# Other start bytes for the stationary operands of a gated feed-forward stage, and for half of its moving ones

## The chip, the cores and the metric

The kernel runs on one core of one Trainium2 chip. The metric is the device time of one execution in microseconds (us), the median of several runs. The profile is one profiled execution of the same program.

## The reference, cut to what matters

The input `x` has 2 x 1024 tokens of 256 numbers. Four blocks follow each other, each added to `x`: a cross attention of one head over 154 context rows, a dense feed-forward stage with eight experts, a cross attention of eight heads, and a routed feed-forward stage with eight experts. The stage that the change touches is the second:

```python
def expert_step(acc, w):          # w: Wg (256 x 1024), Wu (256 x 1024), Wd (1024 x 256) of one expert
    wg, wu, wd = w
    h = jax.nn.silu(x @ wg) * (x @ wu)
    return (acc + h @ wd, None)
acc, _ = jax.lax.scan(expert_step, jnp.zeros_like(x), (Wg, Wu, Wd))   # 8 experts, all tokens
x = x + jnp.tanh(g_ffn[0]) * acc
```

All of it is float32.

## The kernel before

**Tiling.** The 1024 inner columns of each expert are cut into four quarters of 256, which makes 32 quarters in all, and the 2048 tokens into two pairs of 1024. A quarter with a pair is a group: 64 groups, numbered `n`, run one after the other, mostly both pairs of a quarter in a row. Gate and up (`X` is "g" or "u") of a group are not the eight block products each that the plain scheme needs, but seven (`product1` to `product7`) of sums of blocks. The weight blocks and their sums stand in `w_hi` and `w_lo` (two sets, used by even and odd quarters, written by GpSimd), the token blocks and their sums in `xop_hi` and `xop_lo` (one set for each pair, written once).

**Three matmuls for one product.** Each float32 operand is split into a high part rounded to float32r and the rest, and a product is three float32r matmuls of 128x128 by 128x512, from the function `three`:

```python
mm(ps, w, a, ...)        # L1400  high stationary, high moving
mm(ps, w, a_low, ...)    # L1401  high stationary, low moving
mm(ps, w_low, a, ...)    # L1402  low stationary, high moving
```

Each `mm` becomes a load of the stationary operand (LDWEIGHTS, PEld in the profile) and a MATMUL that streams the moving operand. In 64 groups, gate and up take 14 products each, that is 896 products. `down` and `down_seven` multiply the hidden blocks by `Wd`: 484 products, whose stationary operands are `wd_hi` and `wd_lo` (two sets again) or, in 28 groups that use seven products here too, also `wds_hi` and `wds_lo`; the moving ones are `hid_hi` and `hid_lo`, of which even groups use set 0 and odd groups set 1, and `t_hi`, `t_lo`. Together this is 1380 products and 4140 matmuls of one shape.

**Other engines.** VectorE adds halves, multiplies gate by up, subtracts for `hid_lo` and adds the results of down into `acc`. ScalarE applies silu, moves halves and rounds `hid_hi`. GpSimd prepares the weights of the next quarter while the present one is multiplied. SyncE issues the loads. TensorE's order is written out by hand in a loop over `n`, in which the steps of down for group `n - 1` stand between the products of group `n`.

**Places in memory.** Tiles are laid out by `Arena.take`, which gives each a start at the next multiple of 32 bytes in every partition. `align(OPERANDS_AT)` goes on to the next multiple of 2048. In the kernel before, every stationary and every moving operand of the 4140 matmuls begins at a multiple of 64 bytes, and every moving one at a multiple of 2048, since the sizes of all tiles between them are multiples of 2048 or of 512. The stationary operands of the query projection in the third block, `Wq_hi` and `Wq_lo`, are float32r too, and begin 32 bytes behind a multiple of 64; their moving operands `xnT_hi` and `xnT_lo` begin at multiples of 2048 (L1577, L1578, L1582, 96 matmuls of the same shape).

Of the kernel before, what the change touches and what calls it, by code (L numbers as in the profile page):

```python
# [16 lines left out]
F32 = mybir.dt.float32  # L17
F32R = mybir.dt.float32r
# [7 lines left out]
P = 128  # L26
# [63 lines left out]
def flamingo_kernel(nc, x, ctx, mask, g_xattn, g_ffn, W0, b0, Wg, Wu, Wd, gamma, beta, Wq, Wkv, Wout, wgate, We, be, out):  # L90
    B, S, D = x.shape
# [86 lines left out]
    with ExitStack() as stack:  # L178
# [5 lines left out]
        end = nc.sbuf_usable_end // 32 * 32  # L184
# [68 lines left out]
        st = Arena(nc, keep.at, sums_at)  # L253
# [1 line left out]
        half12 = {X: st.take(f"half12_{X}", [P, CH], F32) for X in "gu"}  # L255
        half22 = {X: st.take(f"half22_{X}", [P, CH], F32) for X in "gu"}
        hid = {h: st.take(f"hid{h}", [P, CH], F32) for h in BLOCKS[:2]}
        hid_hi, hid_lo = [], []
        st.align(OPERANDS_AT)
        for i in range(2):  # L260
            hid_hi.append({h: st.take(f"hid_hi{h}_{i}", [P, CH], F32R) for h in BLOCKS})
            if i == 0:
                t3_at = st.at + 4 * CH * BLOCKS.index("12")
            hid_lo.append({h: st.take(f"hid_lo{h}_{i}", [P, CH], F32R) for h in BLOCKS})
# [17 lines left out]
        sb = Arena(nc, sums_at, end)  # L282
# [7 lines left out]
            xop_lo.append(sb.take(f"xop_lo{p}", [P, 7, CH], F32R))  # L290
        xop_end = sb.at
        w_at, w_hi, w_lo, w_raw, wd_hi, wd_lo = [], [], [], [], [], []
        for i in range(2):
            w_at.append(sb.at)
            w_hi.append(sb.take(f"w_hi{i}", [P, 2, 7, P], F32R))
            w_raw.append(Arena(nc, sb.at, end).take(f"w_raw{i}", [P, 2, 7, P], F32))
            w_lo.append(sb.take(f"w_lo{i}", [P, 2, 7, P], F32R))
            wd_hi.append(sb.take(f"wd_hi{i}", [P, 2, D], F32R))
            wd_lo.append(sb.take(f"wd_lo{i}", [P, 2, D], F32R))
        raw_at = sb.at  # L300
        raw_gu = [sb.take(f"raw_gu{i}", [P, 2, KB, FP], F32) for i in range(2)]
        raw_d = [sb.take(f"raw_d{i}", [P, 2, D], F32) for i in range(2)]
# [2222 lines left out]
```

## Time and profile before

| | us |
|---|---|
| median of 3 runs | 1226.97 (1226.01 to 1227.29) |
| the profiled execution's span | 1225.2 |
| TensorE busy | 1199.5 (98%) |
| VectorE busy | 1051.4 (86%) |
| GpSimd busy | 886.6 (72%) |
| ScalarE busy | 739.6 (60%) |
| TensorE's weight loads busy | 987.8 (81%) |

The span runs from the first instruction to the last; the execution's own time beside it is 1226.97 - 1225.2 = 1.8 us longer, going by the median of the runs. A busy MATMUL is counted from its start to its modelled end, which overlaps the next one's start, so its duration is longer than the distance between starts. The distance between two starts is called a step below.

The first attention takes the first 54 us of the span, the dense feed-forward stage from 54 to 999 us, and the last two blocks the rest.

### The profile page before, as it was taken

What the parts mean: (1) busy time and instruction counts of PE and PEld (TensorE: products, weight loads), DVE (VectorE), ACT (ScalarE), POOL (GpSimd) and SP (SyncE); (2) the same over time, 40 slices, a digit from 0 to 9 for tenths busy, and PEclk for the clock granted to TensorE, in tenths of its full rate; (3) what the DMA queues carried; (4) which work ended last, traced back from release to release, by engine and by line L of the source; (5) the groups of instructions that cost most, each with busy time, mean ns of one, the idle gap of its engine ahead of it and who ended that gap; (6) DMA issues with size and microseconds to landing.
All of it is one profiled execution on the core that took longest, in us unless ns stands there. A gap on an engine that the chain in (4) does not pass through costs nothing.

```text
span 1225.2 us, 18428 instructions
## 1 busy us (share of the span) xinstructions
PE 1199.5 (98%) x6143; PEld 987.8 (81%) x6143; DVE 1051.4 (86%) x1754; ACT 739.6 (60%) x1531; POOL 886.6 (72%) x848
## 2 busy tenths in 40 slices
PE   8999999999999999999999999999999998999998
PEld 6778888888888888888888888888888887777776
DVE  6887899999999999999999999999999874767556
ACT  4775566666666666666666666666666545545544
POOL 4575688888888888878888888888888626444435
PEclk9999999999999999999999999999999999999999
DMA  4020301000000000000000000011000330000131
GB/s 142 26 95 25 98 13 39 27 26 26 27 26 27 26 27 26 27 26 27 27 26 27 26 27 26 27 38 40 27 26 1 120 121 1 19 26 11 36 96 70
DMA packets 42365, 48.27 MB, mean 39 GB/s; under 512 B 4239, under 2 KB 40143, under 8 KB 42015
## 3 DMA queue, kind: packets, MB, share of 16 engines
q1 hardware_dynamic: 38992, 43.33, 10.7%
q0 software_dynamic: 1440, 3.41, 0.7%
q8 instruction: 49, 0.80, 0.3%
q10 hardware_dynamic: 1839, 0.37, 0.2%
q14 instruction: 45, 0.37, 0.1%
HBM read 37.36 MB, written 10.29 MB: 39 GB/s over the span
## 4 chain that ended last, share of the span: by engine, by line
PE 89%; DVE 5%; ACT 3%; issue 1%; ACTq 1%; POOL 0%; POOLq 0%; DVEq 0%
PE bank L1400 25%; PE bank L1402 25%; PE bank L1401 25%; ACT PC L1124 3%; PE bank L1643 2%; PE bank L1652 1%; PE bank L1822 1%; DVE nmC L2204 1%; PE bank L1805 1%; PE bank L1345 1%; PE bank L1755 1%; DVE stats L1879 1%; PE bank L1577 1%; PE bank L1627 1%; PE bank L1578 1%
## 5 line engine op out<-in xcount | busy, mean ns | idle before, releaser
L1400 PE MATMUL bank<-xop_hi,w_hi 128*128 128x512 f32 x896 | 349.2, 390 | 1.9 <-DVE half_g L2028 0.9
L1402 PE MATMUL bank<-xop_hi,w_lo 128*128 128x512 f32 x896 | 348.6, 389 | 0.0
L1401 PE MATMUL bank<-xop_lo,w_hi 128*128 128x512 f32 x896 | 348.6, 389 | 0.0
L2063 DVE TENSOR_TENSOR hid_lo<-hid,hid_hi 128x512 fp32r<-128x512 f32 x228 | 232.5, 1044 | 6.0 <-ACT hid_hi L1042 6.0
L1400 PEld LDWEIGHTS bank<-xop_hi,w_hi 128*128 128x128 f32 x896 | 168.2, 188 | 37.9 <-DVE half_g L2028 1.3
L1402 PEld LDWEIGHTS bank<-xop_hi,w_lo 128*128 128x128 f32 x896 | 168.2, 188 | 35.0
L1401 PEld LDWEIGHTS bank<-xop_lo,w_hi 128*128 128x128 f32 x896 | 168.2, 188 | 34.7
L1042 ACT CAST hid_hi<-hid 128x512 fp32r<-128x512 f32 x228 | 140.8, 622 | 63.6 <-PE bank L1402 38.3
L1026 ACT ACTIVATE s<-bank 128x512 f32<-128x512 f32 x128 | 78.2, 611 | 95.2 <-PE bank L1402 95.2
L1400 PE MATMUL bank<-hid_hi,wd_hi 128*128 128x512 f32 x344 | 134.2, 390 | 0.7 <-DVE hid_lo L2063 0.6
L1401 PE MATMUL bank<-hid_lo,wd_hi 128*128 128x512 f32 x344 | 133.9, 389 | 0.0
L1402 PE MATMUL bank<-hid_hi,wd_lo 128*128 128x512 f32 x344 | 133.9, 389 | 0.0
L1002 ACT COPY bank<-bank 128x512 f32<-128x512 f32 x128 | 73.2, 573 | 67.9 <-PE bank L1402 67.9
L2087 DVE TENSOR_TENSOR acc<-bank,acc 128x512 f32<-128x512 f32 x136 | 93.0, 684 | 20.4 <-PE bank L1402 20.3
L1032 ACT ACTIVATE half_g<-half_g 128x512 f32<-128x512 f32 x128 | 81.1, 634 | 46.8 <-DVE half_g L2036 25.5
L2055 DVE TENSOR_TENSOR hid<-half_u,half_g 128x512 f32<-128x512 f32 x128 | 107.2, 875 | 0.0
L702 POOL TENSOR_TENSOR t_loT<-t_rawT,t_hiT 128x512 fp32r<-128x512 f32 x56 | 84.2, 1526 | 16.4 <-ACT t_hiT L1049 16.4
L2046 DVE TENSOR_TENSOR hid<-bank,s 128x512 f32<-128x512 f32 x128 | 86.6, 676 | 1.2 <-PE bank L1402 1.2
L648 POOL TENSOR_TENSOR w_lo<-w_raw,w_hi 128x1024 fp32r<-128x1024 f32 x32 | 77.5, 2421 | 2.9 <-ACT w_hi L1063 2.9
L796 POOL TENSOR_TENSOR PC<-PC,rdenC 128x616 f32<-128x616 f32 x32 | 38.9, 1216 | 53.5 <-DVE rdenC L2212 53.4
L1400 PEld LDWEIGHTS bank<-hid_hi,wd_hi 128*128 128x128 f32 x344 | 64.6, 188 | 15.3 <-DVE hid_lo L2063 1.0
L1402 PEld LDWEIGHTS bank<-hid_hi,wd_lo 128*128 128x128 f32 x344 | 64.6, 188 | 13.5
(288 smaller groups left out, 2608.3 us busy)
## 6 DMA issues: line engine op xcount, KB each, us to landing
raw_gu<-in_L_ffn_Wg_dram SPq DMA_DIRECT2D x32, 256.0 KB, 2.7
raw_gu<-in_L_ffn_Wu_dram SPq DMA_DIRECT2D x32, 256.0 KB, 3.1
raw_d<-in_L_ffn_Wd_dram SPq DMA_DIRECT2D x32, 256.0 KB, 3.6
slots<-empty_row SPq DMA_DIRECT2D x1, 2080.0 KB, 11.2
xr<-slots SPq DMA_DIRECT2D x8, 260.0 KB, 4.5
x_res<-in_x_dram SPq DMA_DIRECT2D x4, 512.0 KB, 8.9
x_mid<-x_res SPq DMA_DIRECT2D x1, 2048.0 KB, 7.4
x_res<-x_mid SPq DMA_DIRECT2D x4, 512.0 KB, 5.4
```

The lines of the kernel that those rows point to most:

```text
L648: nc.gpsimd.tensor_tensor(out=lo[:, :, W_S1:W_S4 + 1], in0=s[:, :, W_S1:W_S4 + 1], in1=hi[:, :, W_S1:W_S4 + 1].bitcast(F32), op=ALU.subtra ...
L702: nc.gpsimd.tensor_tensor(out=t_lo[i][:], in0=t_raw[i][:], in1=t_hi[i][:].bitcast(F32), op=ALU.subtract).then_inc(t_ready, 1)
L1026: nc.scalar.activation(out[:], ps[:], ACT.Silu).then_inc(silu_ready[h], 1)
L1032: nc.scalar.activation(half["g"][:], half["g"][:], ACT.Silu).then_inc(silu_ready[h], 1)
L1042: nc.scalar.copy(hid_hi[n % 2][h][:], hid[h][:]).then_inc(hi_ready[h], 1)
L1400: mm(ps, w, a, start=start, stop=False, skip_group_check=True)
L1401: mm(ps, w, a_low, start=False, stop=False, skip_group_check=True)
L1402: return mm(ps, w_low, a, start=False, stop=True, skip_group_check=True)
L2046: nc.vector.tensor_tensor(out=hid[h][:], in0=ps[:], in1=s[:], op=ALU.mult).then_inc(hid_ready[h], 1)
L2055: nc.vector.tensor_tensor(out=hid[h][:], in0=half["u"][:], in1=half["g"][:], op=ALU.mult).then_inc(hid_ready[h], 1)
L2063: nc.vector.tensor_tensor(out=hid_lo[n % 2][h][:], in0=hid[h][:], in1=hid_hi[n % 2][h][:].bitcast(F32), op=ALU.subtract).then_inc(lo_ready ...
L2087: nc.vector.tensor_tensor(out=to, in0=ps, in1=to, op=ALU.add).then_inc(acc_added, 1)
```

## The change

No instruction is added, removed or moved on any engine, and no semaphore. Tiles begin at other bytes.

- `w_hi`, `w_lo` and `w_raw` are taken with a few elements more: a start of 4 or 12 elements (`HI_AT`) or 8 or 0 (`LO_AT`), and 2 elements (8 bytes) between the gate half and the up half (`SIDE_PAD`).
- `wd_hi` and `wd_lo` get starts of 0 or 2 (`D_HI_AT`) and 12 or 1 elements (`D_LO_AT`).
- `hid_hi` and `hid_lo` of set 1 begin 32 bytes later (`MOVING_AT`).

What this makes of the starts, in bytes modulo 64, worked out from the arena (number of matmuls in brackets):

| stationary tile | before | after |
|---|---|---|
| w_hi, both sets, gate / up (1792) | 0 | 16 / 24 |
| w_lo of set 0, gate / up (448) | 0 | 0 / 8 |
| w_lo of set 1, gate / up (448) | 0 | 32 / 40 |
| wd_hi of set 0 / set 1 (372 / 372) | 0 | 32 / 8 |
| wd_lo of set 0 / set 1 (186 / 186) | 0 | 16 / 36 |
| wds_hi, wds_lo (336) | 0 | 0 |

Moving operands: `xop` (2688 matmuls) and `hid` of set 0 and `t` (684) stay at a multiple of 2048; `hid` of set 1 (768) goes to 32 bytes behind one. Behind the weights everything moves on by 160 to 320 bytes: `raw_gu`, `raw_d`, and in the later blocks `k1T`, `Wouts`, `Wkvs`, `Wqs`, `be_hl` and the routing tiles. `Wq_hi`, `Wq_lo` and the `xnT` tiles stay.

```diff
-        hid_hi, hid_lo = [], []
+        hid_hi, hid_lo, MOVING_AT = [], [], (0, 32)
         st.align(OPERANDS_AT)
         for i in range(2):
+            st.at += MOVING_AT[i]
             hid_hi.append({h: st.take(f"hid_hi{h}_{i}", [P, CH], F32R) for h in BLOCKS})
...
         w_at, w_hi, w_lo, w_raw, wd_hi, wd_lo = [], [], [], [], [], []
+        HI_AT, LO_AT, SIDE_PAD = (4, 12), (8, 0), 2
+        D_HI_AT, D_LO_AT = (0, 2), (12, 1)
+
+        def sides(arena, name, dt, first):
+            n = 7 * P + SIDE_PAD
+            flat = arena.take(name, [P, first + 2 * n], dt)
+            return flat[:, first:first + 2 * n].rearrange("p (s n) -> p s n", s=2)[:, :, 0:7 * P].rearrange("p s (b c) -> p s b c", b=7)
+
+        def down_blocks(arena, name, first):
+            flat = arena.take(name, [P, first + 2 * D], F32R)
+            return flat[:, first:first + 2 * D].rearrange("p (f d) -> p f d", f=2)
+
         for i in range(2):
             w_at.append(sb.at)
-            w_hi.append(sb.take(f"w_hi{i}", [P, 2, 7, P], F32R))
-            w_raw.append(Arena(nc, sb.at, end).take(f"w_raw{i}", [P, 2, 7, P], F32))
-            w_lo.append(sb.take(f"w_lo{i}", [P, 2, 7, P], F32R))
-            wd_hi.append(sb.take(f"wd_hi{i}", [P, 2, D], F32R))
-            wd_lo.append(sb.take(f"wd_lo{i}", [P, 2, D], F32R))
+            w_hi.append(sides(sb, f"w_hi{i}", F32R, HI_AT[i]))
+            w_raw.append(sides(Arena(nc, sb.at, end), f"w_raw{i}", F32, LO_AT[i]))
+            w_lo.append(sides(sb, f"w_lo{i}", F32R, LO_AT[i]))
+            wd_hi.append(down_blocks(sb, f"wd_hi{i}", D_HI_AT[i]))
+            wd_lo.append(down_blocks(sb, f"wd_lo{i}", D_LO_AT[i]))
```

## Rows read from the trace of the kernel before

**Rows 1.** The page: busy us (share of the span) and instructions of each engine; the granted clock.

```profile
PE 1199.5 (98%) x6143; PEld 987.8 (81%) x6143; DVE 1051.4 (86%) x1754; ACT 739.6 (60%) x1531; POOL 886.6 (72%) x848
...
PEclk9999999999999999999999999999999999999999
```

**Rows 2.** Busy time of each engine by window, all of the span, then granted clock.

```profile
core 0: us, PE busy (x) PEld busy (x) DVE busy (x) ACT busy (x) POOL busy (x), PEclk, DMA share, GB/s
...
484.90:514.14 29.24, 29.24 (x130) 24.21 (x129) 27.32 (x37) 18.56 (x34) 24.48 (x23) 1.00 0.09 28
...
200.00:800.00 600.00, 600.00 (x2649) 496.82 (x2648) 559.76 (x740) 380.39 (x676) 503.07 (x454) 1.00 0.09 28
```

**Rows 3.** The chain that ended last, by line, as shares of the span.

```profile
by line: PE bank L1400 25.4%; PE bank L1402 25.3%; PE bank L1401 25.3%; ACT PC L1124 2.6%; PE bank L1643 1.7%; PE bank L1652 1.5%; PE bank L1822 1.1%; issue 1.1%; DVE nmC L2204 1.0%; PE bank L1805 1.0%; PE bank L1345 0.7%; PE bank L1755 0.7
```

**Rows 4.** Timeline of TensorE: start us, us, line, operation, tiles.

```profile
499.65 0.39 PE L1400 MATMUL bank<-hid_hi,wd_hi 128*128 128x512 f32 x1
499.87 0.39 PE L1401 MATMUL bank<-hid_lo,wd_hi 128*128 128x512 f32 x1
...
514.61 0.39 PE L1400 MATMUL bank<-hid_hi,wds_hi 128*128 128x512 f32 x1
```

**Rows 5.** Timeline of the weight loads beside them.

```profile
499.65 0.19 PEld L1401 LDWEIGHTS bank<-hid_lo,wd_hi 128*128 128x128 f32 x1
499.88 0.19 PEld L1402 LDWEIGHTS bank<-hid_hi,wd_lo 128*128 128x128 f32 x1
```

**Rows 6.** Line 1401 from 200 to 900 us: duration ns min/median/max.

```profile
L1401 PE MATMUL bank<-xop_lo,w_hi x671: 389/389/389, 200.0 to 899.0; 128*128 128x512 f32 x168
L1401 PE MATMUL bank<-hid_lo,wd_hi x240: 389/389/389, 206.1 to 897.7; 128*128 128x512 f32 x120
```

**Rows 7.** The same for lines of the query projection, whole span.

```profile
L1578 PE MATMUL bank<-xnT_hi,Wq_lo x32: 392/396/398, 1014.4 to 1141.7; 128*128 128x512 f32 x32
L1582 PE MATMUL bank<-xnT_lo,Wq_hi x32: 387/396/397, 1017.9 to 1143.6; 128*128 128x512 f32 x32
```

**Rows 8.** Timeline of TensorE in the first query projection.

```profile
1014.38 0.40 PE L1578 MATMUL bank<-xnT_hi,Wq_lo 128*128 128x512 f32 x1
1014.62 0.40 PE L1577 MATMUL bank<-xnT_hi,Wq_hi 128*128 128x512 f32 x1
...
1017.65 0.40 PE L1578 MATMUL bank<-xnT_hi,Wq_lo 128*128 128x512 f32 x1
```

**Rows 9.** Timeline of TensorE where the dense stage begins.

```profile
54.27 0.39 PE L1401 MATMUL bank<-xop_lo,w_hi 128*128 128x512 f32 x1
54.50 0.39 PE L1402 MATMUL bank<-xop_hi,w_lo 128*128 128x512 f32 x1
...
55.66 0.39 PE L1401 MATMUL bank<-xop_lo,w_hi 128*128 128x512 f32 x1
...
59.96 0.39 PE L1402 MATMUL bank<-xop_hi,w_lo 128*128 128x512 f32 x1
```

**Rows 10.** Line 1401 over the whole span: duration ns min/median/max.

```profile
L1401 PE MATMUL bank<-xop_lo,w_hi x896: 387/389/396, 54.3 to 990.2; 128*128 128x512 f32 x180
```

**Rows 11.** Pieces of the chain in the last block: start us, us, what.

```profile
1074.22 1.74 PE bank L1652 x8
...
1183.56 1.72 PE bank L1805 x4
```

**Rows 12.** Timeline of GpSimd in one quarter.

```profile
504.95 2.41 POOL L648 TENSOR_TENSOR w_lo<-w_raw,w_hi 128x1024 fp32r<-128x1024 f32 x1
508.69 1.29 POOL L692 TENSOR_TENSOR t_rawT<-hid,hid 128x512 f32<-128x512 f32 x1 [1.32 <-DVE hid L2055]
```

**Rows 13.** The page's groups: VectorE's write of `hid_lo`, busy us and mean ns.

```profile
L2063 DVE TENSOR_TENSOR hid_lo<-hid,hid_hi 128x512 fp32r<-128x512 f32 x228 | 232.5, 1044 | 6.0 <-ACT hid_hi L1042 6.0
```

## The prediction

> **What bounds the kernel now.** I read the page's busy shares first: TensorE is busy for 98% of the span, at the full granted clock in every slice but for rounding [rows 1]. The granted clock of 1.00 is the higher of its two levels, 2.4 GHz [rows 2]. From 200 to 800 us TensorE is busy for 600 of 600 us; nothing makes it wait there, and VectorE, the next, is busy for 559.76 [rows 2]. The chain of work that ended last says the same: the three lines 1400, 1401 and 1402 hold 25.4 + 25.3 + 25.3 = 76% of the span [rows 3], 931 us. So the kernel's time is the number of those matmuls by the distance between two of their starts, plus 290 us of other blocks that the change hardly touches.
>
> The step comes out of the timeline. From the start at 499.65 to the one at 514.61 lie 66 matmuls: 14.96 / 66 = 226.7 ns [rows 4]. All 4140 at that step are 938.5 us, which is the stage from 54 to 999 us but for a few waits at its ends. Each has the modelled duration 389 ns, without a spread, whichever tiles it reads [rows 6]; since 389 - 226.7 = 162 ns is the modelled tail, a duration can be read as a step: take 162 off.
>
> **What is in the step.** 512 columns at 2.4 GHz are 213.3 ns, so 13.4 ns of each step are something else. Other matmuls in this trace have much less of that: eight at line 1652 take 1.74 us, 217 ns each, and four at line 1805, with 512 columns in plain float32, take 1.72 us, 430 ns each [rows 11]. At two clock cycles a column the first are 256 x 2 / 2.4 = 213.3 ns and the second 426.7, so both have some 3 to 4 ns on top. They too have a weight load each. What sets the float32r matmuls apart is that they take a column every cycle, that is a moving stream twice as fast, while the next weight load runs: it starts within 0.01 us of the matmul before it [rows 4, 5]. Some 10 ns a step, 4140 x 10 = 41 us in all, may thus be the two reads standing in each other's way. That is a reading, not a row.
>
> **Does the start byte matter?** One place says so. The query projection has the same shape and type, moving operands at a multiple of 2048 like the stage, and stationary ones 32 bytes behind a multiple of 64. Its duration is 396 ns in the median instead of 389 [rows 7], and from 1014.38 to 1017.65 us there are 14 steps: 3.27 / 14 = 233.6 ns [rows 8]. That is 6.9 ns over the stage's step; by the durations it is 7. Other things differ (what the other engines do, the banks), but in the stage no such difference moved a single duration between 200 and 900 us [rows 6].
>
> A second place says that the step is not a constant of the byte. Where the stage begins, all starts are multiples of 64 already, and still the six steps from 54.27 to 55.66 us are 1.39 / 6 = 231.7 ns, while the 19 from there to 59.96 are 4.30 / 19 = 226.3 [rows 9]. The stream needs some matmuls to fall into its even step. On the way single ones are shorter than it: the least duration of line 1401 is 387 ns [rows 10], 2 under the even one, or up to 3 since both are rounded: a step of 224 to 225.
>
> The Trainium skill ("TensorE: Matmul & The Clock Gate", Part 2, Step-by-step: what each phase is for) says that the two reads have independent ports and that loading the next weights does not steal read bandwidth from the running matmul, and gives 215.7 ns for a warm step of 512 columns. By that rule the change would do nothing. The rows speak against it: 226.7 ns here, and 233.6 with another start byte.
>
> **The change, part by part.**
> - Stationary operands. 560 of the 4140 loads stay at 0 (224 of w_lo, 336 of wds), 596 go to 32 (224 of w_lo, 372 of wd_hi), and 2984 to 8, 16, 24, 36 or 40, for which this trace has nothing. If a start of 32 costs what it does in the query projection, the 596 cost 596 x 6.9 = 4.1 us. For the 2984 I bound the step from both sides: 216.7 ns, where the plain float32 matmuls stand [rows 11], and 233.6 [rows 8].
> - Moving operands of odd groups, 768 matmuls, go to 32. If what counts is the distance between the two starts, this is one more shuffle of the same kind; bound by the same two steps: -768 x 10 = -7.7 to +768 x 6.9 = +5.3 us. It is inside the sum for all 4140.
> - Everything at once. 4140 x (216.7 - 226.7) = -41 us at one end, 4140 x (233.6 - 226.7) = +29 us at the other.
> - Writers. GpSimd writes w_hi and w_lo at starts that are multiples of 4 or 8 bytes only. The largest takes 2.41 us, and later in the quarter GpSimd waits for 1.32 us [rows 12]; in all it is busy for 24.48 of 29.24 us [rows 2]. Its work would have to grow by 4.8 us a quarter before it set the pace, so I take nothing. VectorE writes hid_lo with a mean of 1044 ns [rows 13]; only odd groups move, by 32 bytes, and it has 29.24 - 27.32 = 1.92 us to spare in a quarter [rows 2]. Four such writes a quarter fall in the odd group, so each could grow by 0.4 us. Nothing taken.
> - Later blocks. k1T, Wouts and be_hl move by 160 or 320 bytes, all to multiples of 32. They are plain float32, with 3 to 4 ns over their columns wherever they stand; only be_hl is read by 8 float32r matmuls: 8 x 7 ns = 0.06 us. Nothing taken.
>
> **What I choose.** The cost of a step hangs on how two streams meet. With all starts equal, one meeting is repeated 4140 times. With the starts spread, the matmuls of one product (starts 16, 16, 0 for gate, 24, 24, 8 for up in set 0) meet in turn in different ways. The trace shows that meetings cheaper than the even step exist, at 224 to 225 ns [rows 10], and that one start is dearer. I take the cheaper one, the nearest row on that side, at its lower end, because the room below it reaches on to 216.7: (226.7 - 224) x 4140 = 11.2 us. On the profiled execution: 1225.2 - 11.2 = 1214.0 of span, with 1.8 us around it 1215.8 us; against the median of the runs 1226.97 - 11.2 = 1215.8. This is a weak choice, and the range says so.
>
> The Trainium skill ("SBUF — State Buffer", Door 1, on cachelines) has 16-byte lines in this memory. By it, 512 bytes that start off a multiple of 16 touch 33 lines instead of 32. That would be 1902 of the loads; if a line costs 13.4 / 32 = 0.4 ns, the estimate is 0.8 us against the change. No row here shows it.
>
> **The rivals.**
> - Slower: the even step of 226.7 belongs to equal starts and is the good case. Then the 3580 loads that leave 0 step at 233.6 as in the query projection (+24.7 us, 1251.7), or the stream never settles and stays at the 231.7 ns of its first steps, 4140 x 5.0 = +20.7 us, 1247.7 [rows 8, 9]. For it: both measured departures from the settled pattern are dearer. Against: both are single points, and the 32 is only one of seven starts. It decides as soon as the mean over all starts is above 226.7. A mild form, in which only the starts of 32 are dear, ends at 1227 + 4 = 1231. Chance 0.27 together.
> - Much faster: most of the 10 ns goes. Then 4140 x 10 = 41 us and 1186. But VectorE needs 27.32 us a quarter of 129 matmuls, 211.8 ns for each; at a step of 216.7 it would be busy for 98%, and TensorE would begin to wait for sums and hid_lo. So 1186 is the end and 1190 to 1205 the likelier place. Chance 0.2.
> - No change: the query projection is slower for another reason (its neighbours on the other engines, its banks), and the start byte has no part in it: 1227.0. Or gains and losses of the starts cancel to under 0.6 ns a step. Against: the durations in the stage do not react to anything that the other engines do [rows 6]. Chance 0.09.
>
> **How the numbers follow.** The forecast, a gain of 5 to 22 us (1205 to 1222), gets 0.44. With the much faster case, faster by over 0.2% has 0.64; within 0.2% (2.5 us, about what a measurement of this kernel can tell from no change) 0.09; slower 0.27. Of the much faster case I leave out what lies under 1192, of the slower one what lies over 1248, together about 0.2. The range is 1192 to 1248. The likeliest case alone has 1205 to 1222.
>
> **What the profile after would show.** Right: TensorE still busy for all of 200 to 800 us, the durations of lines 1400 to 1402 no longer one value but several, with a mean near 386 to 387 ns, and 4140 of the new steps as the whole difference in the span. The query projection stays at 396. For the slower rival the durations stand at 393 to 396. For no change they are 389 without a spread. For the much faster one they are near 380, and waits of TensorE for VectorE appear in the stage. Wrong in another way: if the steps are unchanged and the time moves, it is a writer, and GpSimd's or VectorE's mean durations would have grown.

## The result, and the profile after

The changed kernel takes 1245.8 us (1244.6 to 1246.47), the one before 1227.13 us beside it. The ratio is 1.0155, with a 95% interval of 1.0143 to 1.0167: slower by 18.7 us, where a gain of 11 was forecast. The time lies inside the stated range of 1192 to 1248, on the other side of no change, and 2 us from what the slower rival gave for a stream that "never settles", 1247.7. The profiled execution's span is 1244.0 us, 18.8 more than before.

The page after, first busy times and the granted clock, then groups; the lines of `three` are now 1413 to 1415, and VectorE's write of `hid_lo` is 2076. Columns as in [rows 1] and [rows 13]:

```profile
PE 1218.1 (98%) x6143; PEld 987.6 (79%) x6143; DVE 1042.1 (84%) x1754; ACT 739.2 (59%) x1531; POOL 870.7 (70%) x848
...
PEclk9999999999999999999999999999999999999999
...
L1413 PE MATMUL bank<-xop_hi,w_hi 128*128 128x512 f32 x896 | 352.8, 394 | 1.7 <-DVE half_g L2041 0.8
L1415 PE MATMUL bank<-xop_hi,w_lo 128*128 128x512 f32 x896 | 353.3, 394 | 0.0
L1414 PE MATMUL bank<-xop_lo,w_hi 128*128 128x512 f32 x896 | 351.9, 393 | 0.0
L2076 DVE TENSOR_TENSOR hid_lo<-hid,hid_hi 128x512 fp32r<-128x512 f32 x228 | 217.9, 969 | 16.9 <-ACT hid_hi L1055 13.4
```

TensorE is the only engine that is busier (1218.1 instead of 1199.5 us). The clock is as before. VectorE's hid_lo is shorter, 969 instead of 1044 ns [rows 13], and GpSimd is busy for 870.7 instead of 886.6 us, so no writer pays for the new starts. Busy time by window and line 1414 from 200 to 900 us, to be held against [rows 2] and [rows 6]:

```profile
200.00:800.00 600.00, 600.00 (x2595) 486.89 (x2594) 543.35 (x726) 372.15 (x662) 480.26 (x441) 1.00 0.08 27
```

```profile
L1414 PE MATMUL bank<-xop_lo,w_hi x657: 387/393/398, 200.9 to 899.9; 128*128 128x512 f32 x165
L1414 PE MATMUL bank<-hid_lo,wd_hi x233: 392/394/400, 208.5 to 899.2; 128*128 128x512 f32 x117
```

TensorE still waits for nothing between 200 and 800 us, but 2595 matmuls fit in where 2649 did. Such a count holds the one or two that run into the window from before it, so the step is 600 us over the count less two, good to 0.1 ns: 226.7 ns before, 231.4 ns after. 4140 x 4.7 ns = 19.5 us, the whole difference and a little more. The duration of one matmul, which was 389 ns without a spread [rows 6], now goes from 387 to 400 ns in this line, with a median of 393 to 394. The cheap meeting that the forecast was built on is there, 387 ns; it is met now and then, and pays for nothing.

### The profile page after: what moved, and what is told of

Same layout as the page of the kernel before. It is cut to its first block, busy times and chain, and to the rows that moved or that the text cites. A ratio compares the mean times of both kernels' runs of the same rounds, so it can differ in the third digit from the quotient of the medians.

```text
span 1244.0 us, 18428 instructions
## 1 busy us (share of the span) xinstructions
PE 1218.1 (98%) x6143; PEld 987.6 (79%) x6143; DVE 1042.1 (84%) x1754; ACT 739.2 (59%) x1531; POOL 870.7 (70%) x848
## 4 chain that ended last, share of the span: by engine, by line
PE 89%; DVE 5%; ACT 3%; issue 1%; ACTq 1%; POOL 0%; POOLq 0%; DVEq 0%
PE bank L1415 25%; PE bank L1413 25%; PE bank L1414 25%; ACT PC L1137 3%; PE bank L1656 2%; PE bank L1665 1%; PE bank L1835 1%; PE bank L1818 1%; DVE nmC L2217 1%; PE bank L1358 1%; PE bank L1768 1%; DVE stats L1892 1%; PE bank L1309 1%; PE bank L1640 1%; PE bank L1590 1%
## 5 line engine op out<-in xcount | busy, mean ns | idle before, releaser
L1413 PE MATMUL bank<-xop_hi,w_hi 128*128 128x512 f32 x896 | 352.8, 394 | 1.7 <-DVE half_g L2041 0.8
L1415 PE MATMUL bank<-xop_hi,w_lo 128*128 128x512 f32 x896 | 353.3, 394 | 0.0
L2076 DVE TENSOR_TENSOR hid_lo<-hid,hid_hi 128x512 fp32r<-128x512 f32 x228 | 217.9, 969 | 16.9 <-ACT hid_hi L1055 13.4
L661 POOL TENSOR_TENSOR w_lo<-w_raw,w_hi 128x1024 fp32r<-128x1024 f32 x32 | 77.2, 2413 | 19.5 <-ACT w_hi L1076 19.5
L1031 ACT COPY half_u<-bank 128x512 f32<-128x512 f32 x64 | 37.6, 588 | 66.6 <-PE bank L1415 66.6
L1414 PEld LDWEIGHTS bank<-hid_lo,wd_hi 128*128 128x128 f32 x344 | 64.6, 188 | 15.0
```

Of the source, the lines that this page charges most:

```text
L661: nc.gpsimd.tensor_tensor(out=lo[:, :, W_S1:W_S4 + 1], in0=s[:, :, W_S1:W_S4 + 1], in1=hi[:, :, W_S1:W_S4 + 1].bitcast(F32), op=ALU.subtra ...
L1413: mm(ps, w, a, start=start, stop=False, skip_group_check=True)
L1414: mm(ps, w, a_low, start=False, stop=False, skip_group_check=True)
L1415: return mm(ps, w_low, a, start=False, stop=True, skip_group_check=True)
L2076: nc.vector.tensor_tensor(out=hid_lo[n % 2][h][:], in0=hid[h][:], in1=hid_hi[n % 2][h][:].bitcast(F32), op=ALU.subtract).then_inc(lo_ready ...
```

## The experiments

All of them change start bytes alone, but for one that changes what a load reads. "Distance" is the start of the stationary operand less that of the moving one. Beside each stream runs the load for the next matmul [rows 4, 5]; whether it is that load's distance or the matmul's own that counts is not settled here, since the two differ only where distances are mixed. The step is read as above from 200 to 800 us.

**1. One half of the change each.** The moving operands alone:

```diff
-        HI_AT, LO_AT, SIDE_PAD = (4, 12), (8, 0), 2
-        D_HI_AT, D_LO_AT = (0, 2), (12, 1)
+        HI_AT, LO_AT, SIDE_PAD = (0, 0), (0, 0), 0
+        D_HI_AT, D_LO_AT = (0, 0), (0, 0)
```

> Only the second half of the change: hid of odd groups (768 of 4140 matmuls) begins 32 bytes behind a multiple of 2048, all stationary operands stay at 0 modulo 64. Theory S (the stream must meet the same relation of starts all the time to settle in its even step of 226.7 ns): the mix of two moving starts is enough to break it in the groups where they occur; mean step between 229 and 231.4 ns, 1236 to 1246 us. Theory B (each matmul has a price by its own pair of start bytes, and the prices add up): only the 768 matmuls change; at the 6.9 ns of the query projection +5.3 us, 1232 us, and all other durations remain 389 ns.

Measured: 1238.35 us, ratio 1.0097 (1.008 to 1.0114), step 229.2 ns. The line of the low moving operand (1414 here too):

```profile
L1414 PE MATMUL bank<-xop_lo,w_hi x662: 387/389/398, 200.8 to 899.4; 128*128 128x512 f32 x166
L1414 PE MATMUL bank<-hid_lo,wd_hi x237: 389/393/398, 208.3 to 898.1; 128*128 128x512 f32 x119
```

The 768 moved matmuls are down's, yet the `xop` matmuls, whose two operands begin where they did, spread from 387 to 398 ns. 11.3 us over 768 would be 15 ns each, twice the dearest price known. The timeline shows the disturbance and its end:

```profile
487.33 0.40 PE L1413 MATMUL bank<-hid_hi,wd_hi 128*128 128x512 f32 x1
489.42 0.39 PE L1413 MATMUL bank<-hid_hi,wd_hi 128*128 128x512 f32 x1
503.70 0.40 PE L1413 MATMUL bank<-hid_hi,wd_hi 128*128 128x512 f32 x1
```

At 487.33 three moved matmuls begin, and six unmoved ones follow: nine steps in 2.09 us, 232.2 ns each. From 489.42 on none is moved, and the 63 steps up to the next moved matmul at 503.70 are 14.28 / 63 = 226.7 ns. Going by all starts from 200 to 800 us, a moved matmul costs 6.6 ns over the even step, which is close to the 6.9 ns that the prediction had; but unmoved ones, up to eight behind the last moved one, cost as much again (3.4 of 6.6 us in this window). So matmuls with another distance disturb those behind them: a price for each matmul by its own bytes (theory B) falls.

The stationary operands alone (`MOVING_AT` = (0, 0), the rest as in the change):

> Only the first half of the change: the stationary operands at their new bytes, all moving ones at multiples of 2048. Theory S: the stream doesn't settle, as in the whole change: 231 ns, 1244 to 1247 us. Theory B: the whole change's +18.7 us less the part of the 768 moved matmuls (up to 5 us): 1240 to 1246 us, and each start byte has a duration of its own.

Measured: 1246.09 us, ratio 1.0157 (1.014 to 1.0174), step 231.4 ns. It costs by itself all that the whole change costs. The two halves don't add up: 11 and 19 us apart, 19 together. Once the even step is gone, there is no second one to lose.

**2. One start for all.** All stationary operands at 32, with `HI_AT` = (8, 0) and the other constants 0, and the sums `wds` moved alike (they now stand behind the `t` tiles, and the tiles after them begin 128 bytes later):

> All 4140 stationary operands at 32 modulo 64, all moving ones at a multiple of 2048, as in the query projection. Theory S: one relation everywhere, so the stream settles in an even step, durations without a spread; nothing in it says which step; 226.7 ns (1227 us) if the query projection is only too short to settle. Theory B: 233.4 ns for each, 1227 + 4140 x 6.7 ns = 1255 us.

Measured: 1254.69 us, ratio 1.0234 (1.0217 to 1.0252), step 233.4 ns.

```profile
200.00:800.00 600.00, 600.00 (x2573) 483.53 (x2572) 535.40 (x719) 369.65 (x658) 483.73 (x440) 1.00 0.08 27
```

```profile
L1419 PE MATMUL bank<-xop_lo,w_hi x651: 395/396/397, 200.7 to 899.3; 128*128 128x512 f32 x163
```

A stream nearly as even as the one before (395 to 397 ns) at another level, and just the one that the query projection has [rows 7]. Theory S had the even stream right and theory B the time, 1255 us. So being even is not what makes a step short.

Both operands at 32:

```diff
-OPERANDS_AT = 0
+OPERANDS_AT = 32
```

> The kernel before with OPERANDS_AT = 32: stationary and moving operands all at 32 modulo 64, so that their distance is 0 as before; Wq comes to 0 and xnT to 32. If the distance of the two starts counts: 226.7 ns and 1227 us. If the stationary start byte alone counts, as the query projection's 32 could mean: 233.4 ns and 1255 us. Theory S with any relation: settled, no spread of durations.

Measured: 1227.32 us, ratio 1.0001 (0.9991 to 1.0012), step 226.7 ns, durations 389/389/389 again. The distance counts; the bytes themselves, moved together by 32, don't.

**3. Other distances modulo 64.** All stationary operands at 16 modulo 64 (`HI_AT` = (4, 12), all others 12), at 8 (`HI_AT` = (2, 10), others 10), at 48 (all 12), and gate at 0 with up 8 bytes on:

> All 4140 stationary operands at 16 modulo 64, all moving ones at a multiple of 2048. The runs so far have 226.67 ns at distance 0 and 233.33 ns at distance 32, both without a spread over 2 ns. Theory D (a constant distance gives one settled step, and a step is dear by the distance): somewhere between, 230.0 ns if it goes linearly, 1241 us; durations of one or two values. Theory B (price of the byte as seen in the mixed kernels, where loads at 16 have 232.1 ns): 1249 us. Below 226.7 ns only if 0 is not the best distance.

> All 4140 stationary operands at 8 modulo 64, all moving ones at a multiple of 2048. Theory D, linear: 228.3 ns, 1234 us, settled. Theory L (only the 16-byte line counts): 226.7 to 227.1 ns, 1227 to 1229 us. Theory B (231.2 ns in the mixed kernels): 1246 us.

> All 4140 stationary operands at 48 modulo 64, all moving ones at a multiple of 2048. If the distance counts modulo 64 and in both directions alike, as 32 and minus 32 did in the query projection, this equals the run with all at 16. If the direction matters, it differs, and one of the two may lie below 226.7 ns. Linear and even: 230.0 ns, 1241 us.

> The kernel before with one thing of the change, the 8 bytes between the gate half and the up half: gate, down and sums at 0 modulo 64, the 1344 up loads at 8, all moving ones at a multiple of 2048. Theory S (any mix unsettles the stream): a mean of 229 to 231.4 ns, 1236 to 1246 us, and spread durations also for loads at 0. Theory B: the 1344 loads alone get dearer, by what the run with all at 8 shows.

Measured: 1249.89 us (ratio 1.0186, 1.0168 to 1.0203; step 232.4 ns) for 16, 1244.31 us (1.0146, 1.0129 to 1.0162; 231.1 ns) for 8, 1244.51 us (1.0143, 1.0126 to 1.016; 230.9 ns) for 48, and 1246.35 us (1.0154, 1.0137 to 1.0172; 231.3 ns) for the 8 bytes between the halves. None has the step that a price growing evenly with the distance would give (theory D: 228.3 ns for 8, 230.0 for 16 and 48), theory L's 226.7 to 227.1 ns for 8 did not come either, and none has one duration for all: in the run with 8, for example, the three lines for `xop` stand at 397, 393 and 391 ns in the median. Two expectations missed: 16 does not lie half way, and it is not 48's equal. Theory B's prices, taken from the mixed kernels, fit here (232.1 ns for 16, 231.2 for 8), but these runs are mixes themselves. The reason is in how I had built them. The padding pushes each following tile on, so that starts equal modulo 64 lie at up to eight values modulo 512. That made the modulus itself the question.

**4. The modulus.** All stationary operands a further 64, 128 or 256 bytes on, exactly, with all tiles between multiples of 512 (`HI_AT` = (16, 0), (32, 0), (64, 0), others 0, `wds` alike):

> All 4140 stationary operands 64 bytes behind a multiple of 512 (before: at a multiple of 512), the moving ones at a multiple of 2048. If only the distance modulo 64 counts, the stream settles at 226.67 ns and the time is that of the kernel before, 1227 us. If a longer period counts, the stream doesn't settle: 231 ns, 1245 us, or it settles at another step, which could lie under 226.67 ns.

> All 4140 stationary operands 128 bytes behind a multiple of 512, the moving ones at a multiple of 2048. Distance 64 gave a settled pair of steps with the mean 233.33 ns, distance 0 gives 226.67. If the period of the relation is 128, this is 226.67 ns and 1227 us again; if it is longer, another settled mean, 233.33 ns (1254 us) the nearest guess.

> All 4140 stationary operands 256 bytes behind a multiple of 512. If the period is 256: 226.67 ns and 1227 us. If it is 512 or more: settled at another mean, about 233.33 ns and 1254 us; a mean under 226.67 ns would be a kernel that beats the one before.

Measured: 1252.45 us (1.0218, 1.0201 to 1.0236; 233.4 ns) for 64, 1249.38 us (1.0192, 1.0175 to 1.0209; 232.4 ns) for 128, 1227.24 us (1.0002, 0.9993 to 1.0012; 226.7 ns) for 256. The line of the low moving operand in the runs with 64 and with 128:

```profile
L1419 PE MATMUL bank<-xop_lo,w_hi x652: 393/393/398, 199.8 to 899.8; 128*128 128x512 f32 x163
```

```profile
L1419 PE MATMUL bank<-xop_lo,w_hi x655: 389/393/405, 199.8 to 899.7; 128*128 128x512 f32 x164
```

and in the run with 256, the even step back:

```profile
L1419 PE MATMUL bank<-xop_lo,w_hi x670: 389/389/389, 200.4 to 898.8; 128*128 128x512 f32 x168
```

With 64 the durations alternate between 393 and 398 ns, which is why the line shown has 393 in the median at a mean step of 233.4 ns. Distances of 0 and 256 are alike, 64 and 128 are not: the even step of 226.7 ns needs a multiple of 256 bytes, not of 64. (That other distances repeat after 256, such as 32 and 288, was not run.) In the kernel before, all stationary operands begin at multiples of 512 and all moving ones at multiples of 2048, so the distance is 0 modulo 256 everywhere.

Exactly 16 and exactly 8, without the drift of the third group. The tiles overlap by the few elements that none reads, so that each begins 16 (or 8) behind a multiple of 512:

```diff
+        def behind(arena, name, dt, n):
+            flat = nc.alloc_sbuf_tensor_at(name, [P, FIRST + n], dt, offset=arena.at)
+            arena.at += 4 * n
+            return flat[:, FIRST:FIRST + n]
```

> All 4140 stationary operands 16 bytes behind a multiple of 512, exactly (the earlier run with 16 had them at 16 modulo 64 but at eight values modulo 512, and didn't settle: 232.3 ns with steps from 225 to 239). If the stream settles whenever the relation modulo 512 is the same everywhere: durations of one to three values, a mean of 226.67 to 233.33 ns, 1227 to 1254 us. If only the line of 16 bytes or the 64 mattered, it looks like the earlier run: 232.3 ns, spread, 1249 us.

> All 4140 stationary operands 8 bytes behind a multiple of 512, exactly. Settled if the same relation everywhere is what counts: one to three values of the duration, mean between 226.67 and 233.33 ns, 1227 to 1254 us; as in the earlier run with 8 modulo 64 (231.1 ns, 1244 us, spread) if it isn't.

Measured: 1254.02 us (1.0226, 1.0209 to 1.0243; 233.4 ns, durations 397/398/398 in line 1409 for `xop_lo`, 394/394/394 and 394/396/396 in the two other lines for `xop`) and 1242.48 us (1.0131, 1.0114 to 1.0147; 230.8 ns, 390/392/398). With 16 the stream is nearly even (and dearer than the 232.4 ns of the mix with 16 above, so the prices read from mixes are not prices of the byte); with 8 it is not, at one and the same distance everywhere. So sameness is neither enough nor the point (theory S in its first form falls): no distance tried but 0 modulo 256 reaches 226.7 ns.

**5. A harmless mix.** Distances of 256 for gate, up and down, and of 0 for the sums (`HI_AT` = (64, 0), `wds` left in place):

> The kernel before with the stationary operands of gate, up and down 256 bytes later and the sums wds left where they are, so that 336 loads have distance 0 and 3804 distance 256 modulo 512. If the relation counts modulo 256, the mix is none: 226.67 ns without a spread, 1227 us. If a mix unsettles the stream whatever its two relations: mean 229 to 231 ns in the groups with seven products in down, 1236 to 1246 us, as with the moving operands of odd groups 32 bytes off.

Measured: 1226.42 us, ratio 1.0 (0.999 to 1.0011), step 226.7 ns.

```profile
200.00:800.00 600.00, 600.00 (x2649) 496.99 (x2648) 559.61 (x740) 380.29 (x676) 502.73 (x454) 1.00 0.09 28
```

```profile
L1414 PE MATMUL bank<-xop_lo,w_hi x671: 389/389/389, 200.1 to 899.1; 128*128 128x512 f32 x168
```

A mix of the distances 0 and 256 costs nothing.

**6. The query projection.** It was the prediction's dear step; does it follow the rule? Twice the kernel before with one line, 32 bytes more and 224 more:

```diff
+        sg.at += 32      # and 224 in the second
         Wq_hi = sg.take("Wq_hi", [P, KB, INNER], F32R)
```

> The kernel before with Wq_hi and Wq_lo at 0 instead of 32 modulo 64. The 96 matmuls of the query projection have distance 0 then. Settled at 226.67 ns: their durations go from 396 to 389 ns in the median, and the span loses at most 96 x 6.7 ns = 0.6 us, less than the measurement can tell. If their 396 ns came from their neighbours or their banks, they stay.

> The kernel before with Wq_hi and Wq_lo 224 bytes later, at multiples of 256. The run with them 32 bytes later had them at 64 modulo 256 and changed nothing, which fits the 233.33 ns that distance 64 gives in the stage. If the relation modulo 256 is the rule here too, the 96 matmuls of the query projection now settle: durations of 389 ns in the median instead of 396, and at most 0.6 us off the span. If they stay at 394 to 396 ns, the query projection has another reason, and its reading in the prediction was luck.

Measured: 1226.51 us (0.9999, 0.9989 to 1.0008) and 1226.16 us (0.9999, 0.9988 to 1.001), no difference in the total, as it had to be. The lines of the query projection with 32 bytes more, where Wq is at 64 modulo 256:

```profile
L1579 PE MATMUL bank<-xnT_hi,Wq_lo x32: 392/397/398, 1014.3 to 1141.7; 128*128 128x512 f32 x32
L1583 PE MATMUL bank<-xnT_lo,Wq_hi x32: 390/394/398, 1017.8 to 1143.6; 128*128 128x512 f32 x32
```

and with 224 more, at a multiple of 256:

```profile
L1579 PE MATMUL bank<-xnT_hi,Wq_lo x32: 389/389/397, 1015.1 to 1142.0; 128*128 128x512 f32 x32
L1583 PE MATMUL bank<-xnT_lo,Wq_hi x32: 388/389/389, 1018.5 to 1143.9; 128*128 128x512 f32 x32
```

The first of these two missed what it had been built for, since a multiple of 64 was aimed at; the second has 389 ns, in another stage with other neighbours. The rule holds there, for a distance of 0 modulo 256 as for 32 and 64.

**7. Is it the load's walk through memory?** Each load reads one element of a partition 128 times instead of 128 in a row:

```diff
+                w, w_low = (v[:, 0:1].to_broadcast([P, P]) for v in (w, w_low))
                 mm(ps, w, a, start=start, stop=False, skip_group_check=True)
```

> The kernel before, but every one of the 4140 weight loads reads the same 4 bytes 128 times instead of 512 bytes in a row, so that the products are not the reference's; number, shape and order of all instructions are as before. If the 13.4 ns on top of the 213.3 ns of columns come from the load's walk through memory beside the moving stream, the step changes, to 216 to 220 ns if the walk was the cost (1183 to 1199 us, less what VectorE then makes TensorE wait). If they belong to float32r matmuls as such, it stays at 226.67 ns and 1227 us.

Measured: 1245.3 us (one run), step 231.1 ns. The three lines for `xop`:

```profile
L1401 PE MATMUL bank<-xop_hi,w_hi x658: 388/388/388, 200.0 to 898.8; 128*128 128x512 f32 x165
L1402 PE MATMUL bank<-xop_lo,w_hi x658: 397/397/397, 200.2 to 899.1; 128*128 128x512 f32 x165
L1403 PE MATMUL bank<-xop_hi,w_lo x658: 396/396/396, 200.4 to 899.3; 128*128 128x512 f32 x165
```

One step of each three is short and two are long, always in the same order, with all starts at a distance of 0.

Neither alternative of the expectation came: the load without a walk is slower than the load with one. So what a load reads does bear on the step, and the step of 226.7 ns is not a constant of float32r matmuls; but the 13.4 ns are not the bare cost of reading 512 bytes beside the stream either. That how the two reads meet is part of it fits this, but is not shown, and the experiment doesn't say more.

## Why the prediction was wrong

**Right.** What bounds the kernel (76% of the chain in three lines, TensorE without a wait), the reading of a duration as a step, and the sum, number of matmuls by change of step. That the start matters: 226.7 ns, or 230.8 to 233.4, at different distances, with no instruction changed. This speaks against the rule of two independent read ports that the Trainium skill states ("TensorE: Matmul & The Clock Gate", Part 2, Step-by-step: what each phase is for), as far as it would have the starts make no difference. That the writers and the later blocks cost nothing: the query projection has kept its duration (395 and 396 ns in the median), and GpSimd's largest write of w_lo has 2413 instead of 2421 ns.

**The step that failed** is "What I choose", the term (226.7 - 224) x 4140 = -11.2 us. The step did not fall to 224 ns but rose to 231.4, +19.5 us. The prediction took the least single duration, 387 ns in [rows 10], for a place that the new starts could hold. After the change 387 ns stands in the trace again, beside 398. In such a stream the short step has long ones around it, and only the mean counts: in the run with the moving operands alone, each of the 40 matmuls of 387 ns from 200 to 800 us stands behind a step of 240 or 241 ns and before one of 230 or 231. The same could be read before the change. The matmul at 54.27 us is one of those with 387 ns (a step of 224, by the starts in the trace), and it is the first of the six whose steps have a mean of 231.7 ns [rows 9]. So the row for the mean was in the prediction, and served for a rival at 0.27 only; against that rival it said that "both are single points, and the 32 is only one of seven starts", while one extreme of a spread was weighed like a mean. That 231.7 and the measured 231.4 ns lie so close is luck in part: other distances and mixes gave 229.2 to 233.4.

**The byte prices.** The estimate of 4.1 us for the loads at 32, and of -7.7 to +5.3 us for the moved operands of odd groups, took each matmul by itself. The moved operands alone cost 11.3 us, outside their bounds. Their own price was about right (6.6 ns each, where the upper bound had 6.9); missing was that matmuls behind them, which weren't moved, became slower too.

**The modulus.** The prediction counted 560 loads as staying at 0. Modulo 256 only the 336 of the sums do; w_lo of set 0 stands at 64 and 72. It hid the property that the kernel before has and the change takes away. Whether 224 loads more or less at 0 would have mattered for the sign, no run shows; 8 bytes on the up half alone, with the drift behind them, already cost 1.5%.

**The rivals.** The slower one was right in its first half: "the even step of 226.7 belongs to equal starts and is the good case". Its mild form, in which only the starts at 32 are dear, is refuted by the result (1245.8 us against its 1231) and by the runs with exactly 8 and 16 (230.8 and 233.4 ns). "No change" falls with the result itself, a ratio of 1.0155 with an interval that begins at 1.0143.

**What stays open.** Why a distance of 0 modulo 256 is good, why 8 bytes (230.8 ns) are less bad than 16 (233.4), and where the remaining 13.4 ns come from. The experiments show the rule for the even step; they don't show the mechanism, nor whether a matmul's own load or the next one's is the partner that counts. Distances between those tried, such as 4, 96 or 192 bytes, were not run, and none of those tried beats 226.7 ns. The kernel before is the best of them.

## What to carry to other kernels

Where float32r matmuls of 512 columns run back to back, compare the starts of the stationary and the moving operands: in this kernel they must be equal modulo 256 bytes, for each matmul and its neighbours, or the mean step is 1 to 3% longer (229.2 to 233.4 ns instead of 226.7). A padding that only looks at 32 or 64 bytes can lose that for every tile behind it, as in the third group. And where a trace shows a spread of durations, take its mean: the shortest one is no offer.

## What the runs showed of the hardware

- The step of a 128x128 by 128x512 float32r matmul with its weight load, at the upper clock level: 226.7 ns at distances 0 and 256; 230.8 at 8; 232.4 at 128; 233.4 at 16, 32 and 64. With mixed distances 230.9 to 232.4 ns, and 229.2 where only the 768 moved matmuls of odd groups differ.
- The bytes themselves didn't matter in the one case tried: 32 and 32 is 226.7 ns like 0 and 0.
- The disturbance is carried on: with 768 matmuls at another distance, unmoved ones go from 389 ns to anything from 387 to 403, up to eight behind the last moved one; then the even step of 226.7 ns is back.
- With weight loads that read one address 128 times the mean step was longer, 231.1 ns instead of 226.7, in a fixed order of durations of 388, 397 and 396 ns.
